# A Mamba layer with a routed feed-forward on one core: the program's head is written in a new order

## What is computed

```
x_norm = layer_norm(_ln_c(x))
xz     = x_norm @ in_proj_w.T                  # 128 + 128 channels: xi, z
u      = silu(causal_conv4(xi) + conv_b)       # 4 taps along the sequence
dt, Bm, Cm = split(u @ x_proj_w.T)             # 4 + 16 + 16
delta  = softplus(dt @ dt_proj_w.T + dt_proj_b)
h      = exp(delta * A[n]) * h + (delta * u) * Bm[n]     # for n in 0..15, along 1024 tokens
y      = sum_n h * Cm[n] + u * D
y      = (y * silu(z)) @ out_proj_w.T + skip_scale * x_norm
y      = layer_norm(y) @ proj_w.T + proj_b
out    = x + y, and to that a top-1 mixture of 8 experts (64 -> 256 -> 64, capacity 640 tokens each)
```

## Time and profile before

| | us |
|---|---|
| median of 3 timed executions | 437.55 (436.81 to 438.28) |
| the profiled execution, its own time | 436.07 |
| its span, first to last instruction | 434.4 |
| VectorE busy in it | 323.7 (75%) |
| PE busy in it | 328.3 (76%) |
| POOL busy in it | 263.5 (61%) |
| ScalarE busy in it | 224.7 (52%) |

### The profile page before, as it was taken

One profiled execution on the slowest core, in us unless ns is written; L12 is line 12 of the kernel. 1 busy time (PEld: TensorE's weight loads), 2 busy tenths in 40 slices (PEclk: granted clock), 3 DMA queues, 4 the chain that ended last, 5 costly groups with the idle time before them and its releaser, 6 DMA issues. The chain is left out here.

```text
span 434.4 us, 4297 instructions
## 1 busy us (share of the span) xinstructions
PE 328.3 (76%) x1285; PEld 186.6 (43%) x1285; DVE 323.7 (75%) x367; ACT 224.7 (52%) x381; POOL 263.5 (61%) x201
## 2 busy tenths in 40 slices
PE   1755299765699984579989468887657699999990
PEld 0331143222545451274535134443223468878770
DVE  4037999999999997999898798799778126534542
ACT  1346657791666776355778527454432145453520
POOL 7124766679366668489564868657945402666562
PEclk9976589998889998958999697998898769999995
DMA  5991998887577885378986226896893360000000
GB/s 132 172 173 45 368 375 271 276 297 271 188 240 279 274 309 203 115 248 289 318 273 227 72 85 171 242 286 191 148 263 107 102 157 5 3 19 13 16 4 12
DMA packets 44306, 78.60 MB, mean 181 GB/s; under 512 B 16419, under 2 KB 22339, under 8 KB 44282
## 3 DMA queue, kind: packets, MB, share of 16 engines
q1 hardware_dynamic: 41450, 73.88, 55.6%
q0 software_dynamic: 2832, 4.44, 4.4%
HBM read 72.30 MB, written 7.41 MB: 184 GB/s over the span
## 5 line engine op out<-in xcount | busy, mean ns | idle before, releaser
L437 POOL TENSOR_TENSOR prod<-h,csb 128x1024 f32<-128x1024 f32 (+1 forms) x80 | 155.2, 1947 | 80.4 <-DVE h L1081 59.1
L835 PE MATMUL Yp<-prod,ident 128*128 128x512 f32 x256 | 136.3, 656 | 35.5 <-POOL prod L437 35.4
L1081 DVE TENSOR_TENSOR_SCAN h<-dA,Bp 128x1024 f32<-128x1024 f32 (+1 forms) x64 | 128.7, 2016 | 4.0 <-POOL prod L437 0.6
L607 ACT ACTIVATE dA<-delta,aneg 128x1024 f32<-128x1024 f32 (+1 forms) x80 | 76.8, 972 | 53.0 <-DVE delta L1050 27.2
L835 PEld LDWEIGHTS Yp<-prod,ident 128*128 128x128 f32 x256 | 47.6, 204 | 96.4 <-POOL prod L437 57.9
L1059 DVE TENSOR_TENSOR Bp<-Cp,bsb 128x1024 f32<-128x1024 f32 x48 | 59.2, 1232 | 1.7
L495 POOL DMA_INDIRECT out_dram<-dA,h x20 | 20.0, 1001 | 31.7 <-DVE dA L1245 26.8
L467 POOL DMA_INDIRECT slots<-rows_,slot x28 | 29.4, 1049 | 7.7 <-issue 6.3
L1066 DVE TENSOR_TENSOR Bp<-Cp,bsb 128x1024 f32<-128x1024 f32 x16 | 19.7, 1233 | 7.9 <-DMA bsb<-bc_rows 6.8
L1231 DVE TENSOR_TENSOR dA<-Bp,b2s 128x320 f32<-128x320 f32 x8 | 3.9, 492 | 25.4 <-PE Bp L961 25.4
L1081 DVE TENSOR_TENSOR_SCAN h<-dA,hl,Bp 128x512 f32<-128x512 f32 x16 | 20.2, 1274 | 2.1 <-POOL prod L437 1.5
(11 more groups left out here) (234 smaller groups left out, 527.1 us busy)
## 6 DMA issues: line engine op xcount, KB each, us to landing
bsb<-bc_rows SPq DMA_DIRECT2D x48, 512.0 KB, 5.3
csb<-bc_rows SPq DMA_DIRECT2D x48, 512.0 KB, 5.5
bsb<-bc_rows SPq DMA_DIRECT2D x32, 256.0 KB, 4.6
csb<-bc_rows SPq DMA_DIRECT2D x32, 256.0 KB, 4.4
slots<-fill POOLq DMA_DIRECT2D x1, 2600.0 KB, 18.3
h<-slots SPq DMA_DIRECT2D x4, 325.0 KB, 4.2
csb<-slots SPq DMA_DIRECT2D x3, 325.0 KB, 6.3
xs_in<-in_x_dram SPq DMA_DIRECT2D x1, 768.0 KB, 10.0
```

Source lines behind the costliest of these rows:

```text
L437: po.tensor_tensor(prod[:, k % 4, c], h[:, k % 3, c], csb[:, k % CSLOTS, c], ALU.mult).then_inc(s_pP, 1)
L607: ac.activation(dA[:, k % 3, c], delta[:, c], ACT.Exp, scale=aneg[:, n:n + 1]).then_inc(s_dA, 1)
L835: ins = te_.matmul(Yp[:, HB[q]], idn, prod[:, k % 4, HB[q]], start=False, stop=(n == 15), skip_group_check=True)
L1081: ve.tensor_tensor_scan(h[:, k % 3, c], dA[:, k % 3, c], Bp[:, :] if whole else Bp[:, HB[n % 2]], hl[:, n:n + 1] if v == CARRY + 1 else 0. ...
```

## The change

All of it is in the head, save two transfers that leave it. The parts:

1. **Loads.** Five counters in place of three: `w_first` (2 loads: in-projection, taps), `w_cols` (3 columns), `w_dt` (4, for delta), then the other sequences' `x`, then `w_in` (9 that are left). The expert weights (`late`) are issued in unit 0 behind step 13's load of B. The fill of the slots is issued by POOL behind its second product.
2. **First norm.** For sequence 0 the mean is subtracted and the scale applied on VectorE, the inverse root is Ln and Exp on ScalarE. POOL keeps, for the other three, the squares and the last multiplication. The multiplication of taps goes to POOL, the copies out of PSUM of `tapA`, `tapB`, `wzT` to ScalarE.
3. **PE.** Four matmuls whose results nobody reads (`idle`) run before and between the weight transposes. The product for delta (`wdt`) has its own small chain and runs directly behind the convolution. The other products come last.
4. **Rows B and C** are computed ahead of delta's matmuls, taken out of PSUM on VectorE and stored.
5. **Softplus** of sequence 0 in halves of 512 tokens for Exp, 1 + e and Ln. `small` is made on VectorE, max(v, 0) + e on POOL.
6. **Gate**: the Silu of sequence 0's gate moves to unit 0's step 7, where it stands beside sequence 1's.

The diff, cut to its core (lines taken out are shown only where little changes around them; the code printed above has them):

```diff
             sp.dma_start(xs_in[:, 0], x_dram[0]).then_inc(x_first, 16)
+            for dst, src in ((wi[:, :, :], in_proj_w.rearrange("(h p) c -> p h c", p=P)), (cw[:, :], conv_w)):
+                sp.dma_start(dst, src).then_inc(w_first, 16)
+            for dst, src in ((gcol[:, :], ln_g.unsqueeze(1)), (bcol[:, :], ln_b.unsqueeze(1)),
                              (cb[:, :], conv_b.unsqueeze(1))):
+                sp.dma_start(dst, src).then_inc(w_cols, 16)
+            for dst, src in ((dtw[:, :], dt_proj_w), (xdt[:, :], x_proj_w[0:R, :]),
+                             (xbc[:, :], x_proj_w[R:R + 2 * N, :]), (dtb[:, :], dt_proj_b.unsqueeze(1))):
+                sp.dma_start(dst, src).then_inc(w_dt, 16)
+            sp.dma_start(xs_in[:, 1:B], x_dram[1:B].rearrange("b p t c -> p b t c")).then_inc(x_rest, 16)
+            for dst, src in ((alog[:, :], A_log), (Dcol[:, :], D.unsqueeze(1)),
                              (wo[:, :], out_proj_w), (pw[:, :], proj_w), (pb[:, :], proj_b.unsqueeze(0)),
                              (skcol[:, :], skip_scale.unsqueeze(0).broadcast_to([P, 1])),
                              (gw[:, :], gate_w), (gb[:, :], gate_b.unsqueeze(0).broadcast_to([P, E])),
                              (b1r[:, :], b1.rearrange("e (h f) -> (e h) f", h=2))):
                 sp.dma_start(dst, src).then_inc(w_in, 16)
+            def late():
+                for dst, src in ((w1s[0:C, :, :], w1.rearrange("e c f -> c e f")),
...
                     if n == 12 and v + 1 < B:
                         store_rows(v + 1)
+                    if v == 0 and n == 13:
+                        late()
...
+            pool.wait_ge(w_first, 16 * 2)
+            pool.wait_ge(pool_ident, 1)
+            po.tensor_tensor(taps[:, :, :], wi[:, 0, :].unsqueeze(1).broadcast_to([P, TAPS, C]), over(cw[:, :], C),
+                             ALU.mult).then_inc(taps_done, 1)
...
+            pool.wait_ge(w_cols, 16 * 3)
+            pool.wait_ge(w_in, 16 * 9)
+            po.tensor_tensor(cen[:, :], ident[0:C, 0:C], invC[:, :], ALU.subtract).then_inc(w_cen, 1)
+            po.tensor_tensor(gfold[:, 0:C], ident[0:C, 0:C], gcol[:, :].broadcast_to([C, C]), ALU.mult)
+            po.tensor_copy(gfold[:, C:C + 1], bcol[:, :])
+            po.tensor_tensor(diagD[:, :], ident[:, :], Dcol[:, :].broadcast_to([P, P]), ALU.mult)
+            pool.wait_ge(w_cen, 1)
+            po.tensor_tensor(sk[:, :], cen[:, :], skcol[0:C, :].broadcast_to([C, C]), ALU.mult).then_inc(w_fold, 1)
+            rest = fz[:, 1:B].rearrange("p b t c -> p (b t) c")
+            pool.wait_ge(n_xm, 2)
+            po.tensor_tensor(squares[:, T:B * T, :], rest, rest, ALU.mult).then_inc(n_sq, 1)
+            pool.wait_ge(g_rel, 1)
+            pool.wait_ge(f_exp, 2)
+            po.tensor_tensor(trel[:, :], trel[:, :], at(du, 0), ALU.add).then_inc(f_high, 1)
+            pool.wait_ge(n_root, 1)
+            po.tensor_tensor(rest, rest, over(fs[:, 5, T:B * T], C), ALU.mult).then_inc(n_z, 1)
...
+                    if v == 0 and n == 1:
+                        pool.wait_ge(fill_done, 2)
+                        po.dma_start(slots_dram.rearrange("(k p) r -> p k r", p=P),
+                                     fill[:, :].unsqueeze(1).broadcast_to([P, E * ET, ROW])).then_inc(b_sent, 16)
...
+                    act.drain()
+                    ac.activation(at(u, f), at(u, f), ACT.Silu).then_inc(f_silu, 1)
+                    if f == 1:
+                        ac.activation(at(sz, 0), at(sz, 0), ACT.Silu).then_inc(f_gate, 1)
+                    ac.activation(at(sz, f), at(sz, f), ACT.Silu).then_inc(f_gate, 1)
...
+            act_set()
+            act.wait_ge(n_xm, 1)
+            ac.activation(squares[:, 0:T, :], fz[:, 0], ACT.Square).then_inc(n_sq, 1)
+            act.wait_ge(n_var, 1)
+            act.wait_ge(pool_init, 3)
+            ac.activation(fs[:, 3, 0:T], fs[:, 2, 0:T], ACT.Ln, scale=(1.0 + LN_EPS) / C, bias=in_eps[:, :])
+            act.drain()
+            ac.activation(fs[:, 5, 0:T], fs[:, 3, 0:T], ACT.Exp, scale=-0.5).then_inc(n_rstd, 1)
             ac.preload_act_table(ACT.Silu)
+            act.wait_ge(conv_tr, 1)
+            for dst, src in ((tapA[:, :], Cp[:, 0:128]), (tapB[:, :], Cp[:, 128:256]), (wzT[:, :], Cp[0:C, 256:384])):
+                ins = ac.activation(dst, src, ACT.Copy)
+            ins.then_inc(conv_ev, 1)
+            act.wait_ge(w_cols, 16 * 3)
+            for q in range(2):
+                act.wait_ge(f_tr, q + 1)
+                ac.activation(xnT[0:C, 0, 3 + q * HALF:3 + (q + 1) * HALF], bank(0, "norm", q)[0:C], ACT.Identity,
+                              bias=bcol[:, :], scale=gcol[:, :]).then_inc(g_half, 1)
+            for q in range(2):
+                act.wait_ge(f_mx, q + 1)
+                ins = ac.activation(u[:, 0, HB[q]], Yp[:, HB[q]], ACT.Silu, bias=cb[:, :])
+            ins.then_inc(f_silu, 1)
+            act_set()
+            act.wait_ge(w_dt, 16 * 4)
+            for q in range(2):
+                act.wait_ge(f_dt, q + 1)
+                ac.activation(tabs[:, HB[q]], Yp[:, HB[q]], ACT.Abs, bias=dtb[:, :]).then_inc(f_abs, 1)
+            act.drain()
+            for q in range(2):
+                ac.activation(at_half(du, 0, q), tabs[:, HB[q]], ACT.Exp, scale=-1.0).then_inc(f_exp, 1)
+            for q in range(2):
+                act.wait_ge(f_one, q + 1)
+                ins = ac.activation(tabs[:, HB[q]], h[:, 0, HB[q]], ACT.Ln)
+            ins.then_inc(f_ln, 1)
+            ac.activation(te[:, :], at(du, 0), ACT.Square, scale=0.5 ** 0.5).then_inc(f_sq, 1)
...
+            pe.wait_ge(pool_ident, 1)
+            idle(3)
+            pe.wait_ge(w_first, 16 * 2)
+            te_.transpose(Cp[0:C, 256:384], wi[:, 1, :], idn)
+            pe.wait_ge(taps_done, 1)
+            te_.transpose(Cp[:, 0:128], taps[:, 0:2, :].rearrange("p k c -> p (k c)"), idn)
+            te_.transpose(Cp[:, 128:256], taps[:, 2:4, :].rearrange("p k c -> p (k c)"), idn).then_inc(conv_tr, 1)
+            idle(1)
+            pe.wait_ge(n_z, 1)
+            for q in range(2):
+                for t in range(4):
+                    ins = te_.transpose(bank(0, "norm", q)[0:C, t * P:(t + 1) * P], fz[:, 0, 4 * q + t, :], idn)
+                ins.then_inc(f_tr, 1)
+            pe.wait_ge(w_dt, 16 * 4)
+            te_.transpose(Bp[:, HALF:HALF + 2 * N], xbc[:, :], ident[0:2 * N, 0:2 * N])
+            te_.transpose(Bp[0:R, HALF + P:HALF + 2 * P], dtw[:, :], idn).then_inc(dt_tr, 1)
+            pe.wait_ge(conv_ev, 1)
+            for q in range(2):
+                pe.wait_ge(f_top, q + 1)
+                te_.matmul(Yp[:, HB[q]], tapA[:, :], xnT[:, 0, q * HALF:(q + 1) * HALF], start=True, stop=False)
+                te_.matmul(Yp[:, HB[q]], tapB[:, :], xnT[:, 0, 2 + q * HALF:2 + (q + 1) * HALF], start=False,
+                           stop=True).then_inc(f_mx, 1)
+            pe.wait_ge(dt_ev, 1)
+            te_.matmul(Bp[:, 0:P], xdt[:, :], dtwT[:, :], start=True, stop=True).then_inc(dt_mm, 1)
+            pe.wait_ge(f_silu, 1)
+            for q in range(2):
+                te_.matmul((M1, M0)[q][:, :], bcT[:, :, :].rearrange("p k r -> p (k r)"), at_half(u, 0, q), start=True,
+                           stop=True).then_inc(f_bc, 1)
+            pe.wait_ge(dt_ready, 1)
+            for q in range(2):
+                te_.matmul(Yp[:, HB[q]], wdt[:, :], at_half(u, 0, q), start=True, stop=True).then_inc(f_dt, 1)
+            for q in range(2):
+                te_.matmul(Cp[:, HB[q]], wzT[:, :], xnT[0:C, 0, 3 + q * HALF:3 + (q + 1) * HALF], start=True,
+                           stop=True).then_inc(f_mz, 1)
+            pe.wait_ge(w_in, 16 * 9)
...
+            dve.wait_ge(x_first, 16)
+            ve.reduce_sum(fs[:, 0, 0:T], x0, X).then_inc(n_sum, 1)
+            dve.wait_ge(n_sum, 1)
+            ve.scalar_tensor_tensor(z0, over(fs[:, 0, 0:T], C), -1.0 / C, x0, ALU.mult, ALU.add).then_inc(n_xm, 1)
+            dve.wait_ge(n_sq, 1)
+            ve.reduce_sum(fs[:, 2, 0:T], squares[:, 0:T, :], X).then_inc(n_var, 1)
+            dve.wait_ge(n_rstd, 1)
+            ve.tensor_tensor(z0, z0, over(fs[:, 5, 0:T], C), ALU.mult).then_inc(n_z, 1)
+            dve.wait_ge(w_cols, 16 * 3)
+            for q in range(2):
+                dve.wait_ge(g_half, q + 1)
+                ve.tensor_scalar(xnT[C:P, 0, 2 + q * HALF:2 + (q + 1) * HALF], bank(0, "norm", q)[0:C], gcol[:, :],
+                                 bcol[:, :], ALU.mult, ALU.add).then_inc(f_top, 1)
+            dve.wait_ge(dt_tr, 1)
+            ve.tensor_copy(bcT[:, :, :], Bp[:, HALF:HALF + 2 * N].unsqueeze(1).broadcast_to([P, 4, 2 * N]))
+            ve.tensor_copy(dtwT[:, :], Bp[0:R, HALF + P:HALF + 2 * P]).then_inc(dt_ev, 1)
+            dve.wait_ge(x_rest, 16)
+            ve.reduce_sum(fs[:, 0, T:B * T], xr, X).then_inc(n_sum, 1)
+            dve.wait_ge(dt_mm, 1)
+            ve.tensor_copy(wdt[:, :], Bp[:, 0:P]).then_inc(dt_ready, 1)
+            dve.wait_ge(n_sum, 2)
```

(24 more changed lines are left out.)

329 lines of the change are left out of this document (98 added, 231 removed).

## The result

| | before | changed |
|---|---|---|
| median of 4 runs each | 437.91 us | 426.24 us |
| lowest to highest | 436.81 to 439.23 | 425.23 to 427.63 |
| profiled execution, its span | 436.07, 434.4 | 425.27, 423.6 |
| first scan of unit 0 starts | 47.70 | 33.18 |
| first scan of unit 1 starts | 112.13 | 99.57 |

The ratio is 0.9734, with a 95% interval of 0.9689 to 0.978: the change makes the kernel 11.7 us faster. The forecast was 422.9 (418 to 429).

The account below looks back on a forecast made before the run. VectorE was taken to bound the scan, behind an unhidden head of single-engine chains and waits. 436.07 - 15.2 (earlier first scan) + 0.6 (moved transfers) = 421.5 us profiled, 422.9 as median; range 418 to 429.

Parts of the forecast that it names:

- The first norm: Head, sequence 0: the norm split over VectorE and ScalarE is ready at 7.9 us instead of 12.11.
- PE's idle matmuls: Head, PE: three idle matmuls take 5.4, the clock rises at about 7.4, PE is free at 9.0.
- The rival with the clock too late: Head, PE: the filler ends before the clock rises; 5.0 us more, 427.9 in total; chance 0.10.
- Delta and the softplus: Head, after the convolution: delta's matmuls done at 18.8, Exp at 20.7, VectorE's softplus instructions at 22.5.
- Who pays for POOL: Head, softplus: POOL's addition and VectorE's SBUF instructions hold each other up, costing VectorE's path 1.8 of a possible 0 to 1.9.
- the row it was nearest to: POOL's multiplication of 1536 in the trace of before: 3.61 us beside VectorE's two-input instruction, 2.76 alone.
- the rival without a hold: Head, softplus: POOL and VectorE don't hold each other up; 421.1 us in total; chance 0.13.
- the step on the transfers: Unit 0: the moved fill costs 0.6 us; its issue on POOL, the expert weights and the gate's Silu cost nothing.
- the 5.04 row of the prediction: Trace of before: a 5.04 us power beside VectorE's L1205 that slowed nothing visibly, against the lock rule.
- The fill in unit 0: Unit 0, DMA: the moved fill delays loads of B beyond their 8.0 us margin; 0.6 us is paid.
- The middle bound: Unit 0, DMA: fill and loads take turns by packets, the fill lasts 18 us, loads fall 8.6 behind; 0.6 paid.
- From unit 1 on the same distances as before: Scan, a sign to check: from unit 1 on, the distances stay as in the kernel before.

Follow-up runs that it names:

- the second execution: The changed kernel run again without an edit, in the second group: 427.31 us, ratio 0.9749 against the kernel before.
- the second profile of before: The kernel before run again without an edit, for a second profiled execution: 439.53 us, ratio 0.9991.

## Why the prediction was right, and where it was off

The direction, the place and the size hold: the gain is made ahead of the first scan, passes through the scan but for one stall, and 426.24 lies in the range. The forecast of 422.9 was 3.3 too low. Against the profiled execution it was 3.8 (425.27 against 421.5): 0.7 in the head, 1.4 in unit 0 and 1.7 behind it.

*The first norm* was forecast ready at 7.9 and was at 7.96. That the two agree is in part luck: the chain took 4.27 instead of 4.0 (the subtraction with a scalar operand 0.84, not 0.62; the multiplication 0.69, not 0.62; Ln 0.30; the handoffs 0.1 less in sum), but x was there at 3.69 instead of 3.92.

*PE's idle matmuls.* The three took 5.49 (5.4 forecast), the rise came between 7.4 and 7.9, and the transposes of the input started at 8.74 (9.0). The convolution started at 11.27 (11.1) and the Silu ended at 15.68 (15.3). That the rise came just ahead of the transposes was not safe: in the old head three such matmuls took 4.79 and 4.31 instead of 5.49, so the rise does not come after the same work each time. The rival with the clock too late, filler in place, was priced at 5.0; no run shows that case. The kernel without filler lost only 2.3 to 2.6, because the norm's transposes then start earlier (8.12) and the high level is there at the convolution's fourth row.

*Delta and the softplus.* The others' input was in before 12.28 (12 forecast). Exp ended at 21.38 instead of 20.7: 0.4 of it came with the Silu, 0.2 with PE's four matmuls behind it (3.7 from 15.73 to 19.43, 3.5 forecast), and less than 0.1 with ScalarE (1.15 for the two halves of Exp, 1.1 forecast).

*Who pays for POOL.* 1.8 was taken and 2.03 measured, between L1201's 2.72 and the 0.69 that it takes with the addition gone from POOL. The step was right, and so was the choice of the row it was nearest to; the rival without a hold is out. The 1.84 that it rests on was wrong, however. It was scaled from a multiplication of 1536, while the same addition for the next sequence stands in the trace of before with 2.34, and each product of 1024 with 2.35, not the 1.84 that the step on the transfers uses; beside an idle VectorE the addition took 2.33 (the fill in the head). That the price came out close is in part luck, for VectorE lost less than POOL's whole addition. The rule of the Trainium skill ("SBUF — State Buffer", section "SBUF: two separate sides"), a lock held for a whole instruction, fits these rows: VectorE's 0.69 ends 0.56 behind POOL's 2.52. It leaves the 5.04 row of the prediction unexplained, and no run here looks at that. The first scan started at 33.18, **0.7 later than the 32.5 of the sum**.

*The fill in unit 0* is **the term that was mis-sized**: 0.6 forecast, 1.96 measured (2.7 in the second execution, by the wait). The middle bound, turns by packets, counted 18 us for the fill and a lag of 8.6 of the loads against a margin of 8.0. The fill lasted 22.7. For the load of step 8, issued at 47.57, the multiplication was free to start at 60.86 (62.88 - 2.02), 13.3 later, as forecast; its data was there 15.3 after its issue instead of 5.3. The Trainium skill's round-robin between queue rows ("DMA: Bandwidth & Descriptors", section "Queues, rings and completion order") may be how they share, but the price was not got by it: worked out with the packet times of two transfers that did not run together, it fell 1.4 short. The runs with the fill in pieces settle that it is this transfer, and the run with the fill in the head that nothing else in unit 0 waits.

*The end.* "From unit 1 on the same distances as before" held to unit 3 within 0.4. Behind it the profiled change is 2.1 longer than the profiled before; the second profile of before is as long as the change, so this is at most in part the change's, and the 1.7 by which the forecast is short there stays open.

One thing the prediction left unsaid. It named the wait of 13.78 for the last small weight as the gap, and took it out by reordering the consumers. It used the fill's place only for the landing of one load. The run with only the fill moved shows that this move alone takes 7.2 to 8.95 us out of the head, about half of what there is; with the fill put back, the reordered head loses 6.0, all of it because POOL's addition stands behind the last small weight. The order of consumers and of loads, the filler and the later issue of the expert weights bring the other 7.4 together (40.55 to 33.18). Of these only the filler was run by itself, and without the fill's move it brings nothing.

## What to carry to other kernels

A long wait for a tiny load is a question about what else was in the queues at that time, before it is one about who consumes it: look at the queue engine's own issue times, and try moving the large transfer alone. Where the transfer goes next, spread it over the idle of the DMA, a piece every second step here, since its density is what the loads feel. Work that is given to POOL beside VectorE's critical instructions is not free; give it only what finds VectorE idle or waiting for PE.

## What the runs showed of the hardware that was not expected

- The hold works both ways and on tiny instructions: POOL's copy of one column took 1.78 beside VectorE's L1189 of 1.75, and 0.18 in the kernel with the fill in the head, where its row stands at 27.98 and VectorE is waiting.
- The issue of a small transfer can hold its queue engine for long, as in the rows of SP with the fill beside it. SP's timeline of the change, at the end of unit 0:

```profile
76.12 0.62 SPq L320 DMA_DIRECT2D w2s<-in_L_ffn_w_dram  x1
76.79 7.94 SPq L320 DMA_DIRECT2D b2s<-in_L_ffn_b_dram  x1
```

The last row stands 7.94 us directly behind the large expert weights. VectorE's timeline shows no wait for B or anything else from there to the end of the unit.
- The gain of a faster clock depends on who waits: the same kind of filler was worth 2.3 to 2.6 at the first scan of the changed head and 1.25 at that of the old one with the fill moved, and nothing in the total of the old one with or without that move.
